# K's norms in a chunked linear-attention kernel: head sums by channel on TensorE, or ScalarE squares with an accumulator on the turned tiles

## The reference

```python
q = _causal_dwconv(x @ Wq, conv_q).reshape(Bx, Lx, NH, HD)   # 4 heads of 64, silu inside
k = _causal_dwconv(x @ Wk, conv_k).reshape(Bx, Lx, NH, HD)
q = q / jnp.linalg.norm(q, axis=-1, keepdims=True)
k = k / jnp.linalg.norm(k, axis=-1, keepdims=True)
...
A = jnp.einsum('bnihd,bnjhd->bnij', Kb, K)    # chunks of 64 tokens, Kb = k * beta
```

## Time and profile before

| | |
|---|---|
| median of 3 runs | 1259.58 us (1258.93 to 1262.52) |
| the profiled execution's own time | 1258.96 us |
| its span, first to last instruction | 1257.2 us |
| mean granted TensorE clock | 0.948 |
| PE busy | 1129.3 us (90%) |
| DVE busy | 697.4 us (55%) |
| ACT busy | 622.1 us (49%) |
| POOL busy | 381.2 us (30%) |

### The profile page before, as it was taken

The page is one execution under the profiler, slowest core; times in us unless marked ns, Lnnn a source line. Parts: engine busy times, 40 slices in busy tenths (PEclk is TensorE's granted clock), DMA queues, the critical chain, the costliest instruction groups (busy, mean ns, idle before and its releaser), DMA issues.

```text
span 1257.2 us, 25606 instructions
## 1 busy us (share of the span) xinstructions
PE 1129.3 (90%) x9320; PEld 969.5 (77%) x9321; DVE 697.4 (55%) x1203; ACT 622.1 (49%) x1117; POOL 381.2 (30%) x328
## 2 busy tenths in 40 slices
PE   2696979998989899987898889999999999999997
PEld 1365768777777778876777778899998999999986
DVE  2767766666766666556679842333333333333377
ACT  2665545656574754562654553344444444444442
POOL 0325352534343322522101201343344334433100
PEclk9888878999998999997999999999999999999998
DMA  3112020202020110334413321111111111111456
GB/s 128 32 53 67 1 76 1 76 10 76 1 84 1 38 31 9 127 119 143 135 43 108 111 85 52 43 47 47 51 50 46 46 50 46 50 55 42 150 192 226
DMA packets 54088, 86.36 MB, mean 69 GB/s; under 512 B 6656, under 2 KB 39296, under 8 KB 53888
## 3 DMA queue, kind: packets, MB, share of 16 engines
q1 hardware_dynamic: 46336, 64.37, 15.9%
q0 software_dynamic: 7680, 20.98, 5.4%
HBM read 60.16 MB, written 25.17 MB: 68 GB/s over the span
## 4 chain that ended last, share of the span: by engine, by line
PE 69%; DVE 18%; ACT 7%; issue 3%; POOL 2%; DMA 1%; SPq 0%; DVEq 0%; ACTq 0%; POOLq 0%
PE ps L1379 25%; PE ps L1359 23%; DVE W L1537 4%; PE ps L1216 4%; PE ps L1206 3%; PE ps L1370 3%; PE ps L1278 2%; PE ps L1285 2%; DVE late_room L1719 2%; PE ps L1437 2%; DVE W L1629 1%; PE ps L1339 1%; POOL W L813 1%; PE ps L1321 1%; DVE W L1887 1%
## 5 line engine op out<-in xcount | busy, mean ns | idle before, releaser
L1359 PE MATMUL ps<-late_room,W 128*128 128x256 f16 x3072 | 359.1, 276 | 27.4 <-DVE late_room L1719 21.2
L1379 PE MATMUL ps<-W,late_room 128*128 (+1 forms) x3264 | 379.4, 277 | 0.0
L1379 PEld LDWEIGHTS ps<-W,late_room 128*128 128x128 f16 x3264 | 324.8, 100 | 42.8
L1359 PEld LDWEIGHTS ps<-late_room,W 128*128 (+1 forms) x3072 | 301.7, 99 | 71.2 <-DVE late_room L1719 26.7
L1082 ACT ACTIVATE ps<-ps 128x512 f32<-128x512 f32 x272 | 158.7, 583 | 355.9 <-PE ps L1359 316.5
L1719 DVE SCALAR_TENSOR_TENSOR late_room<-ps,late_room 128x512 f16<-128x512 f32 x272 | 181.0, 687 | 235.2 <-ACT late_room L1087 220.1
L1087 ACT ACTIVATE late_room<-ps 128x512 f16<-128x512 f32 x272 | 155.7, 595 | 2.5
L1537 DVE SCALAR_TENSOR_TENSOR W<-W 128x512 f32<-128x512 f32 x144 | 122.2, 849 | 9.3 <-ACT W L955 5.9
L1216 PE MATMUL ps<-W 128*128 128x512 f16 x384 | 102.3, 412 | 1.5 <-DVE W L1713 1.5
L936 ACT COPY W<-ps 128x512 f32<-128x512 f32 x112 | 61.1, 589 | 45.2 <-PE ps L1278 33.8
L1959 DVE TENSOR_SCALAR late_room<-ps 128x512 f32<-128x512 f32 x36 | 24.9, 691 | 97.8 <-PE ps L1379 97.8
(11 more groups left out here) (188 smaller groups left out, 1362.5 us busy)
## 6 DMA issues: line engine op xcount, KB each, us to landing
wstage<-in_w_ffn SPq DMA_DIRECT2D x40, 512.0 KB, 3.6
W<-yt_d SPq DMA_DIRECT2D x16, 512.0 KB, 5.9
late_room<-in_x SPq DMA_DIRECT2D x8, 512.0 KB, 4.7
W<-in_x SPq DMA_DIRECT2D x8, 512.0 KB, 4.1
x2n_d<-W SPq DMA_DIRECT2D x8, 512.0 KB, 3.2
base_d<-W SPq DMA_DIRECT2D x8, 512.0 KB, 3.7
late_room<-base_d SPq DMA_DIRECT2D x16, 256.0 KB, 4.3
acc_d<-late_room SPq DMA_DIRECT2D x12, 256.0 KB
```

Source lines behind the costliest of these rows:

```text
L1359: last = pe.matmul(up_bank(n, c)[:, f * XT:(f + 1) * XT], weight(slot, d, hw, cols), x_halves[:, hx, d], start=(q == 0), stop=(q == len(pa ...
L1379: last = pe.matmul(down_bank(b)[:, c * D:(c + 1) * D], hs[b][:, hh, f, c * P:(c + 1) * P], weight(slot, DB + f // 4, hw, cols), start=(q = ...
```

## The change

The `ssq` fill goes, so that the front has 15 fills. ScalarE no longer squares `Kr`; PE no longer sums by head in slot 4; ScalarE no longer copies the sums. In place of these, once PE has turned half h of K into the bank `tokK{h}`, ScalarE squares that bank in eight instructions of 64 columns (two token tiles, four heads), each with an accumulator output into its own column of `ssq`: half 0 in slot 5 between project(0) and silu(4), half 1 at the head of the front's slot 6, ahead of project(1) and silu(5). The pow on POOL is split: 8 columns in slot 5 and 8 in slot 6 instead of 16 in slot 4. DVE's two multiplies wait each for its own pow. The squares themselves are still written to the room of `sqK`, which nothing reads.

```diff
--- before.py
+++ after.py
@@ -129,8 +129,7 @@
 
 
 FRONT_FILLS = (
-    [(f"proj{m}", "act") for m in PROJ_ORDER[:6]]
-    + [("ssq", "act"), (f"proj{PROJ_ORDER[6]}", "act")]
+    [(f"proj{m}", "act") for m in PROJ_ORDER[:7]]
     + [(f"tokK{h}", "dve") for h in range(2)]
     + [(f"proj{PROJ_ORDER[7]}", "act")]
     + [(f"KT{d}", "act") for d in range(DB)]
@@ -799,10 +798,12 @@
             pool.wait_ge(const_in, CONSTS_IN)
 
             def front(slot, n, b):
-                if slot == 4:
-
-                    pool.wait_ge(*fr.empty(n, "ssq"))
-                    pool.tensor_tensor(ssq, ssq, minus_half[:, 0:GT * NH], ALU.pow).then_inc(rnorm, 1)
+                if slot in (5, 6):
+
+                    h = slot - 5
+                    part = ssq[:, 2 * NH * h:2 * NH * (h + 1)]
+                    pool.wait_ge(squares, 4 * NH * n + 2 * NH * (h + 1))
+                    pool.tensor_tensor(part, part, minus_half[:, 0:2 * NH], ALU.pow).then_inc(rnorm, 1)
                 if slot == 9:
 
                     pool.wait_ge(at_kept, n + 1)
@@ -943,9 +944,6 @@
                     act.wait_ge(conv_step, 3 * DB * (TAPS - 1) * n + (TAPS - 1) * (i + 1))
                     at = conv_at(m, b)
                     act.activation(at, at, ACT.Silu).then_inc(silu_done, 1)
-                    if m in (2, 3):
-                        act.wait_ge(silu_done, 3 * DB * n + i + 1)
-                        act.activation(sqK[:, m - DB], at, ACT.Square).then_inc(squares, 1)
 
                 def project(m):
 
@@ -954,6 +952,13 @@
                                    scale=1.0 / (X_SCALE * W_SCALE)).then_inc(pre_ready, 1)
                     act.activation(conv_at(m, b), fr.bank(f"proj{m}"), ACT.Copy,
                                    scale=cw_down[:, m:m + 1]).then_inc(fr.empty(n, f"proj{m}")[0], 1)
+
+                def key_squares(h):
+
+                    act.wait_ge(*fr.full(n, f"tokK{h}"))
+                    for g in range(2 * NH):
+                        act.activation(sqK[:, h, g * HD:(g + 1) * HD], fr.bank(f"tokK{h}")[:, g * HD:(g + 1) * HD], ACT.Square,
+                                       accum_out=ssq[:, 2 * NH * h + g:2 * NH * h + g + 1]).then_inc(squares, 1)
 
                 def gate(d):
 
@@ -984,15 +989,15 @@
                 if slot == 4:
                     silu(3)
                     project(5)
-                    act.wait_ge(*fr.full(n, "ssq"))
-                    act.copy(ssq, fr.bank("ssq")[:, 0:GT * NH]).then_inc(fr.empty(n, "ssq")[0], 1)
                 if slot == 5:
                     if n >= 2:
 
                         act.wait_ge(o_ready, n - 1)
                     project(0)
+                    key_squares(0)
                     silu(4)
                 if slot == 6:
+                    key_squares(1)
                     project(1)
                     silu(5)
                 if slot == 7:
@@ -1228,9 +1233,6 @@
                     project((6, 7, 4)[slot - 1])
                 if slot == 4:
                     project(5)
-
-                    pe.wait_ge(squares, DB * (n + 1))
-                    head_sums(fill(fr, n, "ssq"), sqK).then_inc(fr.sem_full, 1)
                 if slot == 5:
                     project(0)
                     turn_out(fr, n, "tokK0", Kr, 0)
@@ -1547,7 +1549,7 @@
 
                     h = slot - 5
                     name = f"tokK{h}"
-                    dve.wait_ge(rnorm, n + 1)
+                    dve.wait_ge(rnorm, 2 * n + h + 1)
                     dve.wait_ge(*fr.full(n, name))
                     dve.tensor_tensor(heads(Kt[b][:, 2 * h:2 * h + 2]), bank_heads(fr.bank(name)),
                                       by_head(ssq[:, 2 * NH * h:2 * NH * (h + 1)]), ALU.mult).then_inc(fr.empty(n, name)[0], 1)
```

## The result

| | before | changed |
|---|---|---|
| median | 1259.58 us (7 runs, 1255.56 to 1263.65) | 1247.82 us (7 runs, 1245.96 to 1251.67) |
| ratio, 95% interval | | 0.9902 [0.9882, 0.9922] |
| span of the profiled execution | 1257.2 us | 1244.2 us |

The change made the kernel faster by about 12 us, a little under 1%. The forecast was 1264, slower, in a range of 1252 to 1277. Measured again beside the later experiments, the changed kernel gave 1248.49 and the kernel before medians from 1256.7 to 1263.1, so a few us between runs taken at different times say little.

The account below looks back on a forecast made before the run. The start of scaling 1 on VectorE was taken to bound each group; the groups summed to 16 s - 34.5, with s = 2.5 +5.5 us on 1258.96, about 1264.5, given as 1264, range 1252 to 1277.

Parts of the forecast that it names:

- What bounds the kernel now: In the attention half, the chain ending last sets each group through one start on VectorE (341.94 in group 5), not busy shares.
- scaling 1: VectorE's multiply that scales the second turned half of K; its start was claimed to move everything behind it.
- What is removed: Per group: ScalarE's two squares (0.64 each), PE's wait (2.85), head sums (2.25), slow down product part (1.4), sums copy (0.17), 16-wide pow.
- s: Time of one batch of eight 64-column ScalarE squares with accumulator, between K's turning and the pow; 2.5 us, bounds 0.9 to 3.3.
- formulas: Per-group change in the start of scaling 1, from 2s - 1.8 in group 0 to 2s - 7.2 in groups 6 and 7.
- rival 1: On ScalarE between K's turning and key pow, the accumulator costs nothing: s = 1.7, net -6 us, 1253; chance 0.25.
- Group 5 step by step: From project(5) on PE to scaling 1: it starts at 336.3 + 2s against 341.94, 2s - 5.6; 0.6 us won.
- the floor: In group 5, ScalarE's rms spread ends no sooner than 336.6, scaling 1 no sooner than 338.4 + s; binds below s = 2.1.
- The other groups: Same sum elsewhere: groups 0 to 3 lose 3.2, 3.0, 2.7, 2.2 us; group 4 gains 0.6, groups 6 and 7 2.2 each.
- the full-clock branch, 2s - 4.8: Group 3's change in scaling 1 if PE is at full clock; 2s - 0.9 if three pieces take double; midway 2s - 2.8 used.
- The pow: POOL's 8-wide pow per half, between squares and scaling, predicted at 1.7 us, 1.8 with hops to VectorE.
- PE bounding after all: Rival: PE sets each group, so each wins wait and head sums, 41 us together, 1218; chance 0.03.

## Why the prediction was wrong

**What bounds the kernel now.** Right for this change: scaling 1 was the number to follow. Its differences sum to -11.7 us, and just behind the front's last group the chain was 11.4 us earlier. The spans differ by 13.0, so most of the rest of the program only started earlier. That whatever moves scaling 1 moves everything behind is too strong: 2.8 us were given back on the way, and with the key pows first scaling 1 came 1.1 us earlier in a kernel 5.6 us slower.

**What is removed.** The pieces were right. Put back one at a time, the wait and the sums cost 11.2 and 12.8 us.

**s, the unknown: the step that failed.** "0.31 each, **s = 2.5**". Measured 0.20 and 1.65. A batch under 2 us was one of the signs that the prediction had named for being wrong. That a second small operation appears was right. Wrong was the way of pricing it. I took a lone duration (0.21, 0.2) and took off 0.1 once for the pair. In a stream of small instructions every one of them, the read too, costs its start-to-start time, 0.1 us. The row of two 512-wide copies allowed this reading, an overlap for each instruction, and so (0.21 - 0.1) + (0.2 - 0.1) = 0.21; that the read overlaps as well only the trace of the changed kernel shows. With s = 1.65 the prediction's own formulas and floors give +1.5, +1.3, +1.0, +0.5 and then -1.9 twice and -3.5 twice, -6.3 in sum, and 1253, rival 1. The sign hung on this one term. Rival 1, with a chance of 0.25, had the size of the batch (1.7) by luck: its reason, an accumulator that costs nothing, did not hold, since without the reads a batch is 0.7 us shorter. The Trainium skill's figures (ScalarE: Activation LUTs, What ACT_TABLE_LOAD costs) came to 1248 as an estimate and pointed the right way, with the read left out. That this is the measured time is luck: its s of 1.3 is not the 1.65 measured, and the early groups make up for it. The 0.94 us for eight squares without the read is less than the 1.26 us that the figures give.

**Group 5 step by step, and groups 4, 6 and 7.** Right in mechanism and size: the floor binds, and -1.8, -2.0, -3.4, -3.6 were measured where the formulas give -1.9, -1.9, -3.5, -3.5.

**The other groups.** The second miss, 5 us. Measured +0.1, +0.9, -0.2, -1.7. I had project(0) of group 0 at the slow clock (2.6) and put group 3 midway between its two clocks. Both ran at full clock: 1.47 and 1.46 us for project(0). In group 2 project(5) took 1.71 us where the kernel before, and so the sum, had 2.61. These three are about 4 of the 5 us. In group 3 the full-clock branch, 2s - 4.8, gives -1.5 against -1.7 measured. The two runs that put back one part each speak for the small passes as what brought the lower clock in the early groups: with the sums and no wait project(0) took 1.66 and 2.72 us in groups 0 and 2, with the wait and no sums 1.46 or 1.47 in all four.

**The pow.** Right, 1.63 against 1.7.

**Rivals.** PE bounding after all (1218) did not happen, but the run with the sums put back shows that TensorE's time is on the path as far as Y4 and XT3 in the full groups. The rule "the busy shares of PE and ScalarE do not move it" was too strong: in the changed kernel the chain is on TensorE until 331.87.

**Numbers.** The 1264 was 16 us too high, and 1252 as a lower end left out a result of 1247.8: the edge at s = 1.7 carried only rival 1's sum and nothing of the clock in groups 0 to 3, which was worth about 4 us.

## What to carry to other kernels

When a change replaces a wait by serial work, follow one queued instruction behind both and price new small instructions by start to start in a stream, not by their durations. Where an in-order engine stands for a result, first try to move the waiting piece behind independent work of that engine: here this alone, with the old arithmetic, gave 1242, and with K turned in one go and the small passes kept apart 1238, against 1248 for the new arithmetic in its first order and 1237 in its best.

## What the runs showed of the hardware

- ScalarE: a 64-column square from PSUM with an accumulator is an ACTIVATE and an ACTIVATION_READ_ACCUMULATOR, with mean durations of 269 and 254 ns, yet a pair starts every 0.20 us; with 32 columns every 0.18. The recorded durations grow along a batch (0.24 to 0.28) while the starts stay even.
- TensorE: next to each other, the head sums' 32 passes of two columns left the granted clock at 0.63 over the four microseconds at the end of and behind them (1.2 against 2.4 GHz for most of it), and project(0) took 1.9 to 2.6 us in groups 5 to 7, but 1.33 and 1.54 in group 4. The same passes in two groups of sixteen with a product between ran at full clock in all four. A stand of TensorE of about 2 us ahead of the down product, without the sums, was followed by one of 2.79 us in groups 5 to 7 and by one of 4.20 us in group 4.
